# Moving the first w2 weight loads of each expert ahead in GpSimd's queue: attention plus 8-expert MLP on eight cores

## The reference

```python
xn = layernorm(x)                          # x: 8 x 2048 x 1024, f32
# attention: softmax over m of q.k is summed over m and multiplied with v,
opt = einsum('blmh,blhd->blhd', att, v)    # so it equals v: only v and w_out matter
a = opt @ w_out.T + b_out
# experts: E = 8, F = 4096, top 2 of 8
logits = xn @ router_w.T; top2 and softmax of the two values
h1 = gelu(xn @ w1[e].T + b1[e])            # 2048 x 4096 per expert
y  = h1 @ w2[e].T + b2[e]                  # 2048 x 1024 per expert
out = x + a + sum over the top two of weight * y
```

## Time and profile before

| | |
|---|---|
| median of 2 runs | 4067.9 us (4016.78 and 4119.03) |
| the profiled execution, its time | 4016.95 us |
| its span, slowest core (7) | 4015.4 us (the cores: 3998.6 to 4015.4) |
| TensorE matmuls busy | 3768.8 us, 94% of the span |
| ScalarE busy | 606.9 us, 15% |
| GpSimd busy, the writing of its DMA descriptors | 667.8 us, 17% |
| VectorE busy | 357.1 us, 9% |
| w1 loads | 512 of 256 KB in SBUF, 4.2 us to landing (median) |
| w2 loads | 512 of 256 KB in SBUF, 4.1 us to landing (median) |

### The profile page before, as it was taken

One profiled execution on the slowest core, in us unless ns is written; L12 is line 12 of the kernel. 1 busy time (PEld: TensorE's weight loads), 2 busy tenths in 40 slices (PEclk: granted clock), 3 DMA queues, 4 the chain that ended last, 5 costly groups with the idle time before them and its releaser, 6 DMA issues.

```text
span 4015.4 us, 41883 instructions; the slowest of 8 cores (3998.6 to 4015.4 us)
## 1 busy us (share of the span) xinstructions
PE 3768.8 (94%) x17200; PEld 1684.4 (42%) x17200; DVE 357.1 (9%) x626; ACT 606.9 (15%) x569; POOL 667.8 (17%) x1073
## 2 busy tenths in 40 slices
PE   3788999999999999999999999999999999999994
PEld 2333444444444444444444444444444444444441
DVE  5421100000010000000010100100000010100001
ACT  0230030211102020211203011020202112030200
POOL 1111111111111111111111111111111111111110
PEclk9898999999999999999999999999999999999997
DMA  6553554445545545554557355455445545454554
GB/s 115 77 72 42 73 83 66 76 71 76 75 72 75 78 69 72 76 76 71 76 81 153 44 76 75 71 76 77 70 71 76 76 71 76 72 79 69 76 71 105
DMA packets 255705, 307.07 MB, mean 76 GB/s; under 512 B 51687, under 2 KB 182759, under 8 KB 255520
## 3 DMA queue, kind: packets, MB, share of 16 engines
q0 software_dynamic: 248608, 279.23, 48.8%
q1 hardware_dynamic: 6912, 25.17, 1.9%
HBM read 574.89 MB, written 8.39 MB: 145 GB/s over the span
## 4 chain that ended last, share of the span: by engine, by line
PE 90%; DVE 5%; DMA 2%; issue 1%; ACT 1%; DVEq 0%; SPq 0%; ACTq 0%; POOLq 0%
PE P L344 44%; PE P L424 43%; DVE scr L438 3%; PE P L374 1%; PE P L188 1%; DMA x_rot<-x 1%; ACT vg L355 1%; DMA wvw<-wvf 1%; DMA scr<-x 1%; DVE scr L519 0%; DVE scr L516 0%; PE P L229 0%; DVE x_rot L468 0%; PE P L380 0%; DVEq L46 0%
## 5 line engine op out<-in xcount | busy, mean ns | idle before, releaser
L424 PE MATMUL P<-wvw,vg 128*128 128x512 bf16 x8192 | 1818.5, 383 | 66.3 <-DVE scr L438 50.5
L344 PE MATMUL P<-xnF,wvw 128*128 128x512 bf16 x8192 | 1777.2, 380 | 13.4 <-ACT optF L197 7.1
L424 PEld LDWEIGHTS P<-wvw,vg 128*128 128x128 bf16 x8192 | 803.9, 99 | 1078.5 <-issue 149.4
L344 PEld LDWEIGHTS P<-xnF,wvw 128*128 128x128 bf16 x8192 | 800.5, 98 | 985.7 <-issue 28.0
L355 ACT ACTIVATE vg<-P,b1c_sb 128x1024 bf16<-128x1024 f32 x512 | 570.5, 1114 | 3046.9 <-PE P L344 3046.5
L401 POOL DMA_DIRECT2D wvw<-w2r x512 | 360.0, 705 | 1595.8 <-PE P L424 1523.7
L327 POOL DMA_DIRECT2D wvw<-w1r x512 | 271.6, 533 | 1498.8 <-PE P L344 1495.5
L438 DVE SCALAR_TENSOR_TENSOR scr<-P,wmap_sb,scr 128x512 f32<-128x512 f32 x256 | 192.1, 750 | 3253.5 <-PE P L424 3229.4
L188 PE MATMUL P<-xnF,wvw 128*128 128x512 bf16 x256 | 78.6, 466 | 35.4 <-DMA wvw<-wvf 20.2
L229 PE MATMUL P<-scr 128*128 128x128 f32 x128 | 23.9, 349 | 66.4 <-DVE scr L220 66.4
L188 PEld LDWEIGHTS P<-xnF,wvw 128*128 128x128 bf16 x256 | 27.6, 114 | 78.3 <-issue 63.0
(11 more groups left out here) (41 smaller groups left out, 107.4 us busy)
## 6 DMA issues: line engine op xcount, KB each, us to landing
wvw<-w1r POOLq DMA_DIRECT2D x512, 256.0 KB, 4.2
wvw<-w2r POOLq DMA_DIRECT2D x512, 256.0 KB, 4.1
scr<-x SPq DMA_DIRECT2D x16, 512.0 KB, 4.8
wvw<-wvf POOLq DMA_DIRECT2D x32, 256.0 KB, 5.4
x_rot<-x SPq DMA_DIRECT2D x16, 512.0 KB, 5.5
out<-x_rot SPq DMA_DIRECT2D x16, 512.0 KB, 3.8
wo_sb<-wo POOLq DMA_DIRECT2D x8, 256.0 KB, 13.1
b1c_sb<-b1c POOLq DMA_DIRECT2D x1, 128.0 KB, 14.6
```

The lines of the kernel that those rows point to most:

```text
L344: pair=pair: t.matmul(pair[:, j * 512:(j + 1) * 512], w1sl[:, sl * 1024 + fc * 128: sl * 1024 + fc * 128 + 128], xnF[:, fc * T + half * 10 ...
L424: t.matmul(W2B[tl], vg[:, f1c * 1024 + tl * 128: f1c * 1024 + (tl + 1) * 128], w2sl[:, sl * 1024 + (f1c % 2) * 512: sl * 1024 + (f1c % 2) ...
```

## The change

Issuing a w2 load becomes a function, `issue_w2_load`, that remembers what it has issued and does nothing the second time. It is called from three places: as before, at each group of `emit_w2`; after h1's group 2 (chunks 4 and 5), for the first four groups of the first sweep of the same expert, in all expert stages of half 1 and in those of experts 1 to 7 in half 0; and at the end of the first sweep, for the first four groups of the second. TensorE's wait for a w2 load now uses the count remembered for that load. What is loaded, and into which slot, stays the same.

```diff
--- before.py
+++ after.py
@@ -360,6 +360,9 @@
     def emit_h1(half, e):
         for g in range(NF1C // 2):
             emit_h1_group(half, e, g)
+            if g == 2 and (half == 1 or e >= 1):
+                for g2 in range(4):
+                    issue_w2_load(half, e, 0, g2)
 
     def emit_outproj(half):
         p.wait("tensor", "dwo", 16 * NFC)
@@ -388,24 +391,34 @@
                 mixed[:, tl * 1024:(tl + 1) * 1024], pair), inc="dve")
             set_pair(tl % 2, "dve", tok_oev[(half, tl)])
 
+    w2_ord = {}
+
+    def issue_w2_load(half, e, hh, g):
+        key = (half, e, hh, g)
+        if key in w2_ord:
+            return
+        sl = g % 4
+        if tok_w2use.get(sl) is not None:
+            p.wait("gpsimd", "pe", tok_w2use[sl])
+        elif DO_B and sl >= 2:
+            p.wait("gpsimd", "pe", tok_vpmm[(3, 7)])
+        nw2[sl] += 1
+        w2_ord[key] = nw2[sl]
+        p.do("gpsimd", lambda gg, e=e, g=g, hh=hh, sl=sl: gg.dma_start(
+            w2sl[:, sl * 1024:(sl + 1) * 1024].rearrange(
+                "p (c n) -> p c n", c=2),
+            d_w2[e, 2 * g:2 * g + 2, :, hh * 512:(hh + 1) * 512].rearrange(
+                "c p n -> p c n")),
+            inc=DW2[sl], inc_by=16)
+
     def emit_w2(half, e):
         for hh in range(2):
             sweep = (half, e, hh)
             for g in range(NF1C // 2):
                 sl = g % 4
-                if tok_w2use.get(sl) is not None:
-                    p.wait("gpsimd", "pe", tok_w2use[sl])
-                elif DO_B and sl >= 2:
-                    p.wait("gpsimd", "pe", tok_vpmm[(3, 7)])
-                nw2[sl] += 1
-                p.do("gpsimd", lambda gg, e=e, g=g, hh=hh, sl=sl: gg.dma_start(
-                    w2sl[:, sl * 1024:(sl + 1) * 1024].rearrange(
-                        "p (c n) -> p c n", c=2),
-                    d_w2[e, 2 * g:2 * g + 2, :, hh * 512:(hh + 1) * 512].rearrange(
-                        "c p n -> p c n")),
-                    inc=DW2[sl], inc_by=16)
+                issue_w2_load(half, e, hh, g)
                 for f1c in (2 * g, 2 * g + 1):
-                    p.wait("tensor", DW2[sl], 16 * nw2[sl])
+                    p.wait("tensor", DW2[sl], 16 * w2_ord[(half, e, hh, g)])
                     p.wait("tensor", "act", tok_gelu[(half, e, f1c)])
                     for tl in range(8):
                         if f1c == 0:
@@ -448,6 +461,9 @@
                         tok_w2use[sl] = tok
                     tok_w2_reader[f1c] = tok
             last_sweep[0] = sweep
+            if hh == 0:
+                for g2 in range(4):
+                    issue_w2_load(half, e, 1, g2)
 
     def emit_final(half):
         for tl in range(8):
```

## The result

The change is 0.27% slower: the ratio to the kernel before is 1.0027, with a 95% interval from 1.0016 to 1.0038. On 4016 us that is 11 us (6 to 15). The profiled execution took 4023.86 us, against 4016.95.

What follows compares the result with a forecast made beforehand. The prediction took TensorE's matmuls as the bound, busy 3768.8 of 4015.4 us, with no weight load in the chain. It summed 4016.95 + 0 + 0 + 1 = 4018 us, range 4003 to 4070.

Steps and rivals of the forecast that it cites:

- nothing is gained at w2's start: Start of w2 after h1: the w2 loads already landed 3.1 us before use, so issuing them earlier gains 0.
- the 13.7 us of the Gelu: TensorE's waits after 377 us for the last Gelu of an h1: 13.7 us, to stay unchanged.
- Rival B: At w2's start, the 13.7 us put down to the Gelu are really w2 load waits and vanish: 4003 us, chance 0.03.
- the call at the sweep's end: Between sweeps 0 and 1, the four loads stand at the same place behind the same waits: cost and gain 0.
- the changed count: TensorE's wait for each w2 load: each load keeps its number, so the wait is the same: 0.
- The landing at the 14 other places: Chunk 6's w1 load behind the moved burst in h1: lands 8.0 us after issue, 1.9 us before needed, cost 0.
- The rule that the w1 load has to let the w2 bytes through: DMA rings consume descriptors in order: chunk 6's w1 landing is 8.0 us with it, nearer 4.2 without; cost 0 either way.
- R1: Rival from the experiments, not the prediction: each of the 15 moved bursts costs some tenths of a microsecond; no chance given.
- I take 1 us, once, with 0 and 4 as bounds: Half 1, expert 0, beside SyncE's transfers: chunk 6's w1 load in time or some 0.7 us late, 1 us taken.
- rival A: Moved loads starve chunk 6 at all 15 places: 39 us, up to 4057 us, chance 0.10; beyond 2%, 0.03.
- Within 2%: Whole kernel: time stays within 2% of before, covering the forecast, B and the small A; chance 0.95.
- the forecast's own range: Whole kernel: 4008 to 4028 us, 0.3% for differences between executions, around the forecast that had chance 0.82.

Runs made afterwards that it cites:

- only this call: Kernel before with just one burst of four w2 loads moved, that of half 1, expert 0, plus the call at the first sweep's end: ratio 1.0020 (1.0006 to 1.0034).
- the 14 other bursts: The change without its call after group 2 in half 1, expert 0, against the kernel before: ratio 1.0008, timed again 1.0003 (0.9993 to 1.0012).
- SyncE's transfers held back: The whole change, but in half 1, expert 0 SyncE's stores and loads wait until chunk 5 ends; against the kernel before: ratio 1.0001 (0.9989 to 1.0013).
- the transplanted traffic: The change without its half 1, expert 0 call, with added SyncE x loads in half 0, experts 2 to 5: 4042.1 and 4041.9 us, kernel before 4014.4.

## Why the prediction was right and where it failed

**That nothing is gained at w2's start: right.** The loads were early before, and the 13.7 us of the Gelu are 13.7 us still. Rival B is out: nothing was hidden in them.

**That the call at the sweep's end and the changed count do nothing: not contradicted.** The sweeps and the waits between them are as they were. They had no kernel of their own; "only this call" and "the 14 other bursts" both contain them, and the latter is at 1.0003.

**The landing at the 14 other places: right.** It was worked out as 8.0 us after the issue, 1.9 us before it is needed. Expert 3 of the changed kernel, all w1 loads issued from 957 to 985 us:

```profile
DMA to landing us min/median/max: 4.2/4.4/8.0
```

The largest is chunk 6's. At the 14 places on the eight cores of this kernel it landed after 7.3 to 10.5 us, 8.1 in the median. The rule that the w1 load has to let the w2 bytes through, on which 8.0 in place of 4.2 hung, is what the run shows: at every place and on every core this w1 load landed after the last of the four w2 loads. The 1.9 us of reserve were nearly enough, but not on each core at each place (3 of these 112 landings took more than 9.97 us); the waits that follow, mostly under 1 us and 2.9 at the longest (with SyncE's transfers held back, core 2), are the rest of R1. So the term of these places was not quite the 0 of the sum. Why one core is hit and its neighbour not was not found out.

**"I take 1 us, once, with 0 and 4 as bounds": this step failed.** The place and the mechanism were right, the term was mis-sized. It was to be 0.7 us late and was 4.25 us late, over the upper bound, and 6.65 us in all with the slow clock; the 2.4 us of clock had no term at all in the sum. (By the prediction's own numbers the load is some 0.5 us late and not 0.7, and rival A's 39 us give 4056 and not 4057; neither matters.) Two errors account for a part of the 4.25.

- The rate. The working took 277 GB/s from a stretch of 4 us in which no w2 load ran, and applied it to 13 us with a burst of them. The changed kernel's stretches give 249, 175, 177 and 309 GB/s, 228 in the mean, with the engines full. At 228 the upper end of the wanted bytes, 3.7 MB, takes 16.2 us in place of 13.4: from 2104.80, when chunk 5's load goes out, to 2121.0, where 2118.07 was needed.
- The kind of bytes. The same rows already held 184 GB/s for a burst of w1 and w2 loads alone. GpSimd's loads convert from f32, so each byte landed stands for two read, and SyncE's don't. The changed kernel's view by queue, for 2105 to 2121 us (packets, MB, share of the 16 engines), has GpSimd's queue first and SyncE's second:

```profile
q0 software_dynamic: 1495, 1.79, 72.2%
q1 hardware_dynamic: 496, 1.84, 36.2%
```

About the same bytes took the engines twice as long on GpSimd's queue. SyncE's 1.84 MB in 36.2% of 16 us are 318 GB/s. Priced each at its own rate, an estimate, the six loads (1.57 MB at 184) and the four transfers (2.1 MB at 318) come to 8.5 + 6.6 = 15.1 us, and a landing at 2119.9, 1.8 us late. The measured 2122.07 is 2.2 us later still. A part of that may be chunk 4's w1 load, which landed only at 2106.34 and is in neither count; the rest is open. Both errors were worked out after the result; no run separates them.

**The clock.** A wait priced as its own length holds only while it is short. Here every wait of 3.7 us and more cost another 1.5 to 2.9 us, and some shorter ones, from 2.0 us on, did too.

**The verdict.** "Within 2%" was given 0.95 and holds. The time also lies within the forecast's own range, 4008 to 4028, but that is luck: the range stood for noise around no loss. The forecast itself was no change but one microsecond, 4018 us, and the measured change is a loss that its interval separates from nothing. Of the rivals, A comes nearest, with a starved chunk 6; but it starves at one place, and A had put it at all 15.

No version here beats the kernel before, and the runs point to none: the w2 loads were never waited for, so the best that moving them to this place can do is to cost nothing.

## What to carry to other kernels

Before a load is issued earlier, ask whether anything waited for it; if nothing did, the move can only lose, and what it can lose is the reserve of the load that now stands behind it. Size that reserve for the place with the most other traffic and not for the typical one: two streams that cost nothing clear of noise each (1.0000 and 1.0003) cost some 7 us where they met. Price queued bytes at the rate measured for their own kind over a stretch as long as the queue, and add to a wait of some microseconds what the clock takes behind it.

## What the runs showed of the hardware

- A w1 load behind four w2 loads on GpSimd's queue landed after all four of them, every time (15 places, the eight cores of the changed kernel). It took 7.3 to 10.5 us where nothing of SyncE ran beside them, and 12.6 to 15.0 us where SyncE moved 1 MB at a time, against 4.2 us unhindered. With SyncE's loads only beside it (the transplanted traffic) it took 11.5 to 17.7 us.
- A full set of DMA engines moved 175 to 309 GB/s as counted in these stretches, by what it moved. GpSimd's converting loads took 72.2% of the engines for 1.79 MB, counted as landed, and SyncE's transfers 36.2% for 1.84 MB.
- With a wait of 3.7 us or more TensorE always ran at the 1.2 GHz level for a while, at 1.5 to 2.9 us of cost; with waits of 2.0 to 3.6 us it did so in six cases of 16, and with shorter ones never.
